# First loads of a conditional-LoRA residual layer: each from a connected region of memory instead of from the strided rows of one packed array

## The reference

```python
def reference(x, itok_B_0_7, L0_cond_W, L0_cond_Wr, L0_cond_A, L0_cond_B):   # x: (64, 32, 512)
    base = einsum('btd,od->bto', x, W)                       # W: (512, 512)
    logits = einsum('btd,ed->bte', x, Wr)                    # Wr: (8, 512)
    logits = logits + (one_hot(language_ids, 8) * 5.0)[:, None, :]
    topw, topi = top_k(logits, 2)
    weights = softmax(topw, axis=-1)
    gates = sum(one_hot(topi, 8) * weights[..., None], axis=-2)
    h = einsum('btd,erd->bter', x, A)                        # A: (8, 16, 512)
    lora_out = einsum('bter,bte,eor->bto', h, gates, B)      # B: (8, 512, 16)
    return x + base + 2.0 * lora_out
```

## Time and profile before

| what | us |
|---|---|
| three executions: median (lowest to highest) | 80.47 (80.07 to 80.56) |
| the profiled execution, its own time | 80.74 |
| its span, first to last instruction | 78.9 |
| TensorE busy | 75.4 (95% of the span), 505 matmuls |
| VectorE, ScalarE, GpSimd busy | 48.8, 22.1, 22.6 |
| 16 DMA engines, mean over the span | 180 GB/s, 14.23 MB |

### The profile page before, as it was taken

How to read it: one execution, slowest core, us unless ns; L and a number is a source line. 1 busy time by engine, 2 the same in 40 slices (tenths; PEclk the granted TensorE clock), 3 DMA queues, 4 the chain that set the end, 5 groups by cost and what they waited for, 6 DMA issues and landing times.

```text
span 78.9 us, 1629 instructions
## 1 busy us (share of the span) xinstructions
PE 75.4 (95%) x505; PEld 71.4 (90%) x505; DVE 48.8 (62%) x220; ACT 22.1 (28%) x56; POOL 22.6 (29%) x26
## 2 busy tenths in 40 slices
PE   6999999999999999999999999999999999999960
PEld 2388799899999999999999999999999999999950
DVE  0095695888892828466482928275664829787750
ACT  4423961244231414050231314140503214112100
POOL 4032926061550241406050513305060605100000
DMA  1999995389199289999930000270000053031133
GB/s 12 293 263 362 412 425 237 40 324 408 37 252 423 121 224 428 423 282 349 411 143 6 0 0 0 97 302 0 0 0 0 0 249 149 0 133 77 60 133 133
DMA packets 3892, 14.23 MB, mean 180 GB/s; under 512 B 432, under 2 KB 1328, under 8 KB 3632
## 3 DMA queue, kind: packets, MB, share of 16 engines
q1 hardware_dynamic: 3744, 13.98, 48.4%
q10 hardware_dynamic: 144, 0.20, 0.7%
HBM read 9.99 MB, written 4.19 MB: 180 GB/s over the span
## 4 chain that ended last, share of the span: by engine, by line
PE 87%; DMA 7%; SPq 1%; ACT 1%; DVE 1%; issue 0%
PE heads_ps L421 43%; PE base_ps L421 28%; DMA first_sb<-in_first 7%; PE heads_ps L453 5%; PE base_ps L453 5%; PE base_ps L457 2%; PE heads_ps L457 2%; PE ghT_ps L444 2%; ACT x_hi L231 1%; SPq L165 1%; DVE out_sb L337 1%; SPq L164 0%; PE warm_ps L444 0%
## 5 line engine op out<-in xcount | busy, mean ns | idle before, releaser
L206 POOL TENSOR_TENSOR x_lo<-xT_sb,x_hi 128x512 fp32r<-128x512 f32 x14 | 18.1, 1294 | 38.8 <-ACT x_hi L241 37.0
L421 PE MATMUL heads_ps<-w_hi,x_hi 128*128 128x392 f32 x64 | 22.8, 366 | 0.2 <-ACT x_hi L231 0.2
L421 PE MATMUL heads_ps<-w_hi,x_lo 128*128 128x392 f32 x64 | 21.6, 348 | 0.0
L421 PE MATMUL heads_ps<-w_lo,x_hi 128*128 128x392 f32 x64 | 21.1, 339 | 0.0
L421 PE MATMUL base_ps<-w_hi,x_lo 128*128 128x256 f32 x64 | 17.8, 281 | 0.0
L421 PE MATMUL base_ps<-w_hi,x_hi 128*128 128x256 f32 x64 | 17.8, 289 | 0.0
L421 PE MATMUL base_ps<-w_lo,x_hi 128*128 128x256 f32 x64 | 17.4, 280 | 0.0
L287 DVE TENSOR_TENSOR ghT_lo<-ghT_ps,ghT_hi 128x128 fp32r<-128x128 f32 x15 | 4.4, 291 | 14.8 <-ACT ghT_hi L245 14.7
L421 PEld LDWEIGHTS heads_ps<-w_hi,x_hi 128*128 128x128 f32 x64 | 12.0, 192 | 1.2 <-ACT x_hi L231 0.7
L421 PEld LDWEIGHTS heads_ps<-w_hi,x_lo 128*128 128x128 f32 x64 | 12.0, 191 | 0.5 <-POOL x_lo L210 0.5
L245 ACT ACTIVATE ghT_hi<-ghT_ps 128x128 fp32r<-128x128 f32 x15 | 4.1, 275 | 29.5 <-PE ghT_ps L444 29.5
(11 more groups left out here) (43 smaller groups left out, 92.2 us busy)
## 6 DMA issues: line engine op xcount, KB each, us to landing
x_sb<-in_x SPq DMA_DIRECT2D x4, 768.0 KB, 5.5
out<-out_sb SPq DMA_DIRECT2D x4, 768.0 KB, 4.4
xT_sb<-in_xT SPq DMA_DIRECT2D x3, 768.0 KB, 4.3
first_sb<-in_first SPq DMA_DIRECT2D x3, 454.0 KB, 5.8
xT_sb<-in_xT SPq DMA_DIRECT2D x1, 1024.0 KB, 6.3
x_sb<-in_x SPq DMA_DIRECT2D x1, 1024.0 KB, 9.6
out<-out_sb SPq DMA_DIRECT2D x2, 256.0 KB, 2.0
out<-out_sb SPq DMA_DIRECT2D x4, 128.0 KB, 1.7
```

Source lines behind the costliest of these rows:

```text
L206: nc.gpsimd.tensor_tensor(x_lo[:, s, :], xT_sb[:, t - len(FIRST), :], x_hi[:, s, :].bitcast(FP32), ALU.subtract).then_inc(x_lo_made, 1)
L421: return nc.tensor.matmul(dst, xs[:, s, chunks[k]], ws[:, k, cols], start=(k == 0 and n == 0), stop=(k == KC - 1 and n == last_n))
```

## The change

The DRAM array `in_first` is replaced by four arrays: `in_x0` (128 rows of 1,040 B: ids first, then x of chunk 0), `in_wh0` (128 rows of 1,568 B), `in_wb0` (128 rows of 1,024 B) and `in_rest` (chunks 1 to 3, each a region of 128 rows of 3,616 B, one chunk behind the other). Every one of the six loads now reads rows that lie one directly behind the other. In SBUF `first_sb` keeps its size; the four id columns move from behind x to ahead of it, and are loaded for chunk 0 alone, so that a load of chunks 1 to 3 has 16 B less per partition. The number of loads, their order, queues and semaphores, and all computation stay.

```diff
-def cond_resid_program(nc: bass.Bass, first: bass.AP, xT: bass.AP, x: bass.AP,
+def cond_resid_program(nc: bass.Bass, x0: bass.AP, wh0: bass.AP, wb0: bass.AP, rest: bass.AP, xT: bass.AP, x: bass.AP,
                        b: bass.AP, out: bass.AP):
-        first_x = [first_sb[:, k, 0:FIRST_X].rearrange("p (t c) -> p t c", c=P) for k in range(KC)]
-        ids_at = FIRST_X
-        ids_sb = first_sb[:, 0, ids_at:ids_at + 1].bitcast(I32)
-        w_sb = first_sb[:, :, FIRST_X + IDS:]
-        w = first[:, :, FIRST_X + IDS:]
+        first_x = [first_sb[:, k, IDS:IDS + FIRST_X].rearrange("p (t c) -> p t c", c=P) for k in range(KC)]
+        ids_sb = first_sb[:, 0, 0:1].bitcast(I32)
+        w_sb = first_sb[:, :, IDS + FIRST_X:]
-            sp.dma_start(first_sb[:, 0, 0:FIRST_X + IDS], first[:, 0, 0:FIRST_X + IDS]).then_inc(x_landed, 16)
-            sp.dma_start(w_sb[:, 0, base_cols], w[:, 0, base_cols]).then_inc(wb_landed, 16)
+            sp.dma_start(first_sb[:, 0, 0:IDS + FIRST_X], x0).then_inc(x_landed, 16)
+            sp.dma_start(w_sb[:, 0, base_cols], wb0).then_inc(wb_landed, 16)
             for k in range(1, KC):
-                sp.dma_start(first_sb[:, k, :], first[:, k, :]).then_inc(chunk_landed[k - 1], 16)
+                sp.dma_start(first_sb[:, k, IDS:], rest[k - 1, :, :]).then_inc(chunk_landed[k - 1], 16)
-            act.dma_start(w_sb[:, 0, heads_cols], w[:, 0, heads_cols]).then_inc(wh_landed, 16)
+            act.dma_start(w_sb[:, 0, heads_cols], wh0).then_inc(wh_landed, 16)
-        "in_first": np.concatenate([first_x, ids, weights], axis=2),
+        "in_x0": np.concatenate([ids, first_x[0]], axis=1),
+        "in_wh0": np.ascontiguousarray(weights[0, :, :HEADS]),
+        "in_wb0": np.ascontiguousarray(weights[0, :, HEADS:]),
+        "in_rest": np.concatenate([first_x[1:], weights[1:]], axis=2),
```

More of the change, by code:

```diff
@@ L591 @@
     tokens = x.reshape(P, TILES, KC, P)
-    weights = np.concatenate([W[BASE:], A.reshape(ER, D), Wr, W[:BASE]]).reshape(WIDTH, KC, P).transpose(2, 1, 0)
+    weights = np.concatenate([W[BASE:], A.reshape(ER, D), Wr, W[:BASE]]).reshape(WIDTH, KC, P).transpose(1, 2, 0)
     xT = tokens.transpose(3, 1, 2, 0)
     ahead = len(FIRST)
-    first_x = xT[:, :ahead].transpose(0, 2, 1, 3).reshape(P, KC, FIRST_X)
+    first_x = xT[:, :ahead].transpose(2, 0, 1, 3).reshape(KC, P, FIRST_X)
     ids = np.asarray(itok_B_0_7).astype(np.int32).reshape(SEQS).repeat(P // SEQS).view(np.float32)
-    ids = np.broadcast_to(ids.reshape(P, 1, 1), (P, KC, IDS))
+    ids = np.broadcast_to(ids.reshape(P, 1), (P, IDS))
     arrays = {
-        "in_first": np.concatenate([first_x, ids, weights], axis=2),
+        "in_x0": np.concatenate([ids, first_x[0]], axis=1),
+        "in_wh0": np.ascontiguousarray(weights[0, :, :HEADS]),
+        "in_wb0": np.ascontiguousarray(weights[0, :, HEADS:]),
+        "in_rest": np.concatenate([first_x[1:], weights[1:]], axis=2),
         "in_xT": np.ascontiguousarray(xT[:, ahead:]).reshape(P, TILES - ahead, KC * P),
```

## The result

| | before | changed kernel |
|---|---|---|
| median (lowest to highest), 22 executions each | 80.35 us (79.88 to 80.99) | 80.75 us (80.11 to 81.32) |
| ratio | | 1.0041 (95%: 1.0021 to 1.0061) |
| profiled execution, its own time | 80.74 us | 80.64 us |
| span | 78.9 us | 78.8 us |

The change costs 0.4%, 0.33 us by the ratio. I had forecast a gain of 0.23 us. Unless a ratio is said to be over all executions, it leaves out those that took over 1.5% more than the fastest of their kernel, here one of the 22 of the changed kernel. The profiled execution of the changed kernel is a little faster than that of before, so the loss can't be read off the two traces by subtraction. That is the first thing to see here: the executions of one kernel scatter by a microsecond, and each trace is one of them.

What follows compares the result with a forecast made beforehand. TensorE's unbroken work bounds the kernel, its start movable through chunk 1's landing. Issue, bytes and moved ids counted 0, faster reads 0.23 us: 80.47 - 0.23 = 80.24, say 80.25 us; range 79.7 to 80.75 us.

Steps and rivals of the forecast that it cites:

- What bounds the kernel: TensorE, busy 95% of the span, plus its start; first loads matter through chunk 1; chunk 2 to end stays 66.6 us.
- The issue term of 0: SyncE's issue of chunk 1: at worst 0.48 us later for newly opened arrays, but hidden by waiting, so taken as 0.
- The cover of chunk 0: Chunk 0's loads: earlier landing gains nothing behind TensorE's warm-up; later landing is covered for some 0.25 us, then costs one for one.
- Chunk 2 as next limit: If chunk 1 lands earlier, chunk 2's `w_hi`, done at 8.99 us, limits next; unmoved, it allows 0.7 us.
- The cap of 0.96 us: Most that an earlier chunk 1 can gain: 0.31 + 0.65 us of TensorE waiting, chunk 0 being done at 7.02 us.
- the reads themselves: Connected reads of chunks 0 and 1: 12% less time from B against xT, halved to a 0.23 us gain; lower bound 0.
- Rival (d): Chunk 0's loads: engines reading close places hinder each other, landing late; 0.64 us slower, 81.1 us; chance 0.14.
- half the price: Rival (d) with half of its 0.64 us loss from slower chunk 0 loads: 80.8 us.

Runs made afterwards that it cites:

- lengthened kernel: Changed kernel with each of chunk 0's three arrays made longer behind its rows, to 1.86 MB; 79.81 us, 0.9936, and repeated 79.86 us, 0.9917, against the kernel before.
- the one run with a pause in reading: Kernel before, with SyncE issuing chunk 2 and all that follows only after chunk 1 has landed; 82.24 us, 1.0249.

## Why the prediction was wrong

**What bounds the kernel: right.** The time hangs on the first chunks and on nothing behind them. From TensorE's first matmul of chunk 2 to the last sum's start there are 66.6 us before, 66.7 in the changed kernel (9.56 to 76.27, at a mean granted clock of 0.996 where before shows 1.000), 66.6 in the lengthened one (8.30 to 74.91). The packets are 3,744 on SyncE's queue as before. The issue term of 0 was right too: chunk 1 is issued at 1.66 us in both kernels.

**The cover of chunk 0: right as far as it was tried.** In the first profile it landed 0.1 us earlier and nothing came of it; in the second it landed as before.

**Chunk 2 as next limit: right**, and seen in the first profile of the changed kernel, where it lands at 8.3 us and takes back 0.08 us.

**The cap of 0.96 us: too small.** It took 7.02 us as the moment at which TensorE is done with chunk 0. That depends on when the clock rises from the 1.2 GHz to the 2.4 GHz level, by the pace of the matmuls. Before, the heads matmul at 5.66 us still takes 0.33 us and the one at 6.13 us 0.18 us, so it rises at about 6.0 us. In the changed kernel's first profile it rises at about 6.5 us, in its second at 4.7 us, in the lengthened kernel's first at 4.9 us, with the same warm-up in all. In the last two TensorE is done with chunk 0 at 6.3 and 6.46 us, and the lengthened kernel's profiled execution took 79.29 us, 1.45 us less than that of before.

**The term that failed: "the reads themselves".** It was a gain of 0.23 us with 0 as its lower bound; measured, the change loses 0.33 us. I priced the reads at 12% less, from B against tile 2 of xT, two loads that follow others at full rate. That row shows the steady stream, and for chunks 1 to 3 the layout brought little or nothing: connected they gave 0.9997 and 1.0008. I had seen that the first part is slow (0.20 against 0.12 us a packet), but I read the mean as if every packet were somewhat slow. The 87 packets of that row also hold 11 of under 512 B, and the packet records show that most of the large ones take 0.14 us and a few up to 1.1 us; a load lands with its slowest engine. And the term was counted for chunks 1 to 3 and chunk 0 alike, as a price per read, with no loss on any side. The loss came from chunk 0's three small arrays, through the landing of chunk 1 by the estimate above (6.4 to 6.8 us), and not through the reads of chunk 0, which landed no later. What in these arrays makes it is open: the packet records of the one profile of before and those of the changed kernel are alike.

**Rival (d), slower: right in sign, in size half (0.33 of 0.64 us), wrong in place and cause.** Its own figure for half the price, 80.8 us, is near the measured 80.75 us, and that is luck. It had the loads of chunk 0 land late; they landed early or as before. It blamed close rows; the same close rows in longer arrays gave 0.9936 and 0.9917. What the runs show instead is that the size of the arrays of chunk 0 matters, and with it, I take it, how far apart they lie or where each starts. With x's array long the kernel gains; with length added only ahead of chunks 1 to 3 it stays slower. Why this changes the landing of chunk 1, two loads later, was not found. The queue behind, the issues, and the engines' use of SBUF are each excluded by a run as the sole cause of a late landing. Where each array is put in memory no record shows, so "distance" is a reading of the array sizes and not a measured address.

The Trainium skill (DMA: Bandwidth & Descriptors, Latency and other measured facts) has a row in which copies run at half their rate when the rows in memory lie 4 or 8 MB apart, and 4 KB more restore it. There the place in memory decides and not the bytes, which would be of the same kind as what the array sizes do here; its distances are 512 KB and more between rows, and no run here shows that the cause is the same.

**The reading of one trace.** The profile of the changed kernel is 0.1 us better than that of before while the median is 0.4 us worse. Chunk 1's landing in the three profiles of the changed kernel is 6.5, 6.8 and 6.8 us, and before was read from a single late one. Between the two traces the landing moved by 0.28 us and the time by 0.10 us; chunk 2 took back some 0.09 us of it, and the long rest behind was 0.09 us longer. A forecast of 0.23 us on a landing that scatters by more than that was more exact than its base.

## What to carry to other kernels

When the first loads bound a kernel, look at the landing of the slowest DMA engine and at the longest packets, not at the mean rate; and time many executions, since one trace can point the wrong way. Splitting one packed input into small arrays may move whatever lies behind them in memory: try the same kernel with the small arrays padded at their end before judging the layout. Here that turned a loss of 0.4% into a gain of 0.3 to 0.8%, by the one count or the other, and padding x's array alone was enough; 512 KB in place of 1.86 MB was not.

## What was not expected of the hardware

In the first microseconds single packets of 3.6 KB take up to 1.5 us where the usual is 0.14 us. There were 19 to 25 of the long ones in six profiles with short connected arrays for chunk 0 and 24 in the one of the kernel before, and 6 to 14 with long arrays. In the one run with a pause in reading they came back after it (eleven of the first 13 packets). And executions of one kernel spread over 79.2 to 81.1 us (lengthened arrays), of which the time at which chunk 1 lands accounts for nearly all in the traces.
